# A window-attention block on one core: v projected as pairs of half-height matmuls in two banks, and the split of q and k moved behind the parts of the maxima

## The chip, the core and the metric

The kernel runs on one core of a Trainium2 chip. The metric is device time in microseconds. A core has TensorE (PE, matmuls; its weight loads are listed as PEld), VectorE (DVE), ScalarE (ACT), GpSimd (POOL) and SyncE (SP), which here only issues DMAs. Each engine executes its own instructions in the order written, and waits on semaphores for the others.

## The reference

A shifted-window attention block with its MLP, on x of 8 images of 16 x 128 positions and 32 channels; a window is 4 x 32 = 128 positions, an image has 16 windows, there are 4 heads of 8 channels.

```python
y = layernorm(x, g1, b1); y = roll(y, (-2, -2)); xw = windows(y)          # 128 windows of 128 tokens
q, k, v = split(xw @ qkv_w + qkv_b);  q = q * SCALE
attn = einsum('bhid,bhjd->bhij', q, k) + bias + mask
o = einsum('bhij,bhjd->bhid', softmax(attn), v)
x = x + roll(unwindow(o @ proj_w + proj_b), (2, 2))
z = layernorm(x, g2, b2)
return x + gelu(z @ fc1_w + fc1_b) @ fc2_w + fc2_b
```

## The kernel before

All images stay in SBUF with the 128 tokens of a window on the partitions. A **pair** is two windows with their four heads; there are 64 pairs, 8 per image. The loop runs over steps p from -4 to 63, and step p is step s = p % 8 of image b = p // 8. Every engine has its own copy of the loop, written out by hand, and the order of the `if` lines in it is the order of its instructions.

What a step does: TensorE makes the scores of pair p + 4 with rows i on the partitions in ps1 (`bias_s1`, `scores_s1`); VectorE reduces them to negated row maxima (`row_max`, L406), which frees ps1. Every second step TensorE transposes the maxima of two pairs into the first 16 partitions of Q1 (`transpose_max`, L720). ScalarE takes their bfloat16 high part (`high_max`, m_hi, L589), VectorE the rest (`middle_max`, m_mid, L412), and SyncE sends both into the spare rows of q_rows (`send_max`). Two steps later the scores of that pair are made again, transposed, in ps2 (`bias_s2` L758, `scores_s2` L771), with the maxima subtracted by the matmul itself. ScalarE exponentiates them (`exponential`, L594), which frees ps2. TensorE multiplies with v (`weighted_values`, L791), two steps behind.

Beside this runs the preparation of a later image n = b + 2, and the rest of the block for an earlier one. q and k need three bfloat16 parts. In steps 1 and 3 ScalarE takes the high part (`high_part`) of the two halves, from Q1 and Q0. VectorE subtracts it (`remainder`, L397; the first half in step 1, the second in step 4), ScalarE takes the middle part (`middle_part`, L578; steps 2 and 4), GpSimd the low part (`low_part`, L311; steps 2 and 5), and SyncE scatters and gathers them through DRAM. In step 5 TensorE projects v of image b + 1 into Q0 (`project_v`, L708), which has to wait until the second remainder has read Q0, and ScalarE copies it into va (`values`, L583). `wv` is block diagonal: four copies of the 32 x 32 matrix, for four windows side by side in the partitions.

Normalization has a chain of its own: VectorE sums (`means` L367, L369; `variances` L375, L377), GpSimd centres, takes the power for rstd (L297, 2.9 us) and scales, ScalarE squares (L556). After the attention, TensorE turns the outputs around (L859, L865), projects them (L871, after ScalarE's copy onT), and VectorE adds them to x (L428). pq is one PSUM tensor of two banks, Q0 and Q1, shared by the transpositions, the projections of q, k and v and the maxima. After step 63 comes the MLP of all images.

Of the kernel before, what the change touches and what calls it, by code (L numbers as in the profile page):

```python
# [43 lines left out]
def swin_kernel(nc, x, params, rel_i_in, rel_j_in, aux_in, scratch, out):  # L44
# [3 lines left out]
    with ExitStack() as ctx:  # L48
# [313 lines left out]
        def _(dve):  # L362
# [143 lines left out]
            for p in range(FIRST, PAIRS):  # L506
# [7 lines left out]
                if p % 4 == 2 and 0 <= (p - 6) // 4 < OCTETS:  # L514
                    normalize((p - 6) // 4)
                if p >= 0 and n < B and s in (1, 4):
                    remainder(n, s // 4, (Q1, Q0)[s // 4])
                if s == 4 and 0 <= b - 1 < B:
# [6 lines left out]
                if p % 2 == 0 and 0 <= (p + 2) // 2 < GROUPS:  # L525
                    middle_max((p + 2) // 2)
                if 0 <= p + LEAD < PAIRS:
                    row_max(p + LEAD)
# [22 lines left out]
        def _(act):  # L551
# [28 lines left out]
            def values(n):  # L580
                act.wait_ge(vp_done, n + 1)
                after(act, av_done, PPI * (n - 1))
                act.activation(va[:, n % 2, 16:].rearrange("p (n c) -> p n c", c=32)[:, :, 0:HD],  # L583
                               Q0.rearrange("p (n c) -> p n c", c=HD), ACT.Copy).then_inc(va_done, 1)

# [55 lines left out]
            for p in range(FIRST, PAIRS):  # L641
                b, s = p // PPI, p % PPI
                n = b + 2
                if p >= 0 and n < B:
                    if s == 0:
                        copy_yT(n, Q0)
                    if s in (1, 3):
                        high_part(n, s // 2, (Q1, Q0)[s // 2])
                    if s in (2, 4):
                        middle_part(n, s // 2 - 1)  # L650
                if p % 4 == 3 and 0 <= (p - 7) // 4 < OCTETS:
# [15 lines left out]
                if p % 2 == 0 and 0 <= (p + 2) // 2 < GROUPS:  # L667
                    high_max((p + 2) // 2)
                if 0 <= p < PAIRS:
                    exponential(p)  # L670
# [13 lines left out]
        def _(pe):  # L684
# [21 lines left out]
            def project_v(n):  # L706
                for g in range(NG):
                    mm = pe.matmul(Q0[:, 128 * g:128 * (g + 1)], yT[:, n % 2, 128 * g:128 * (g + 1)], wv[:],  # L708
                                   start=True, stop=True)
                mm.then_inc(vp_done, 1)  # L710

            def transpose_max(k):
                pe.wait_ge(max_done, 2 * k + 2)
                if k:
                    pe.wait_ge(mmid_done, k)
                if k % 4 == 2 and 2 <= (k + 2) // 4 + 1 < B:
                    pe.wait_ge(rest_done, 2 * ((k + 2) // 4 + 1) + 1)
                else:
                    pe.wait_ge(yT_done, 2)
                pe.transpose(Q1[0:16, 0:TOK], negm[:, k % 2, :], P("ident")).then_inc(mT_done, 1)  # L720
# [56 lines left out]
            def weighted_values(j):  # L777
                b = j // PPI
                if j % PPI == 0:
                    pe.wait_ge(va_done, b + 1)  # L780
                if j % 4 == 0:
# [93 lines left out]
            for p in range(FIRST, PAIRS):  # L875
# [6 lines left out]
                if p >= 0 and n < B:  # L882
                    if s == 0:
                        pe.wait_ge(va_done, n - 1)
                        after(pe, yT2_done, n - 4)
                        transpose_first(n, Q0)
                    if s == 1:
                        pe.wait_ge(mmid_done, (p - 1 + 2) // 2 + 1)
                        project_qk(n, (Q0, Q1))
                if p % 4 == 2 and 0 <= (p - 6) // 4 < OCTETS:  # L890
                    tokens_first((p - 6) // 4)
                if s == 5 and 1 <= b + 1 < B:
                    if n < B:
                        pe.wait_ge(rest_done, 2 * n + 2)
                    else:
                        pe.wait_ge(yT2_done, b - 2)
                    project_v(b + 1)
                if s == 7 and 0 <= b - 2 < B - 3:
                    pe.wait_ge(va_done, min(b + 2, B))
                    transpose_second(b - 2, Q0)  # L900
# [161 lines left out]
```

## Time and profile before

| | |
|---|---|
| median of 3 runs | 262.0 us (261.79 to 262.4) |
| the profiled execution | 262.69 us, its span 260.9 us |
| granted TensorE clock, mean | 0.99 |
| loop (first row maxima to last) | about 37 to 225 us |

In the rows, a line of the timeline is one run of like instructions: start in us, length in us, engine, line, operation, output <- inputs, count; in brackets the idle time of the engine before it and what ended that. The length of a run of matmuls reaches to its last modelled end, which lies inside the next run, so starts are what one subtracts.

### The profile page before, as it was taken

How to read it: one execution, taken by the hardware profiler on the slowest of the kernel's cores; microseconds unless marked ns; L12 is line 12 of the kernel's file. 1: busy time of each engine (PE TensorE's matmuls, PEld its weight loads, DVE VectorE, ACT ScalarE, POOL GpSimd, SP SyncE). 2: the span in 40 equal slices, each digit the busy share in tenths (PEclk: the TensorE clock that was granted, in tenths of full speed). 3: DMA queues.
4: the chain of work that ended last, by engine and by line, in shares of the span. 5: the costliest groups of instructions: out<-in, count | busy, mean ns of one | idle time of the engine just before them, and what ended most of it. 6: DMA issues, size and time to landing. Idle time of an engine off the chain costs nothing.

```text
span 260.9 us, 8073 instructions
## 1 busy us (share of the span) xinstructions
PE 215.0 (82%) x3336; PEld 122.3 (47%) x3336; DVE 170.0 (65%) x263; ACT 149.1 (57%) x222; POOL 113.3 (43%) x78
## 2 busy tenths in 40 slices
PE   0249105979999999999999999999999998898673
PEld 0116002436656555665666566566566564432221
DVE  5744764577588687858868786777676663384243
ACT  1342800467577566667757766766556566956460
POOL 8462458123630982487098248531600701616000
PEclk9999999999999999999999999999999999999798
DMA  7915443532550542245154124405500000012112
GB/s 225 205 43 184 138 134 101 159 93 91 164 155 19 184 145 89 83 139 158 47 185 142 49 95 154 126 9 183 166 26 5 4 4 1 3 40 83 40 47 113
DMA packets 24843, 26.30 MB, mean 101 GB/s; under 512 B 3732, under 2 KB 22292, under 8 KB 24596
## 3 DMA queue, kind: packets, MB, share of 16 engines
q1 hardware_dynamic: 23704, 24.82, 30.7%
q10 hardware_dynamic: 1104, 0.99, 1.4%
q8 instruction: 26, 0.43, 0.7%
q14 instruction: 9, 0.07, 0.1%
HBM read 17.14 MB, written 8.39 MB: 98 GB/s over the span
## 4 chain that ended last, share of the span: by engine, by line
issue 35%; PE 34%; POOL 19%; ACT 4%; DVE 3%; DMA 3%; ACTq 1%; POOLq 0%; DVEq 0%
POOL rstd L297 6%; PE pav L791 5%; PE ps L758 4%; POOL parts L311 4%; POOL xc L289 4%; PE pav L820 3%; PE ps L771 3%; PE ps L808 3%; PE ps L726 3%; PE pch L832 2%; POOL yn L304 2%; PE pch L871 2%; POOL X L317 2%; ACT prob L594 2%; PE pch L859 2%
## 5 line engine op out<-in xcount | busy, mean ns | idle before, releaser
L406 DVE TENSOR_REDUCE negm<-ps 128x8 f32<-128x1024 f32 x64 | 78.1, 1220 | 32.0 <-PE ps L744 31.9
L594 ACT ACTIVATE prob<-ps 128x1024 f32<-128x1024 f32 x64 | 65.4, 1021 | 28.5 <-PE ps L771 28.5
L297 POOL TENSOR_TENSOR rstd<-var,neghalf 128x16 f32<-128x16 f32 x16 | 46.6, 2913 | 67.9 <-DVE var L377 67.9
L758 PE MATMUL ps<-rel_j,id_b 96*32 96x512 bf16 x512 | 39.9, 385 | 2.3 <-ACT prob L594 2.3
L791 PE MATMUL pav<-prob,va 128*32 128x128 f32 x1024 | 41.0, 279 | 0.0
L726 PE MATMUL ps<-rel_i,ident_b 64*64 64x512 bf16 x256 | 27.4, 418 | 14.1 <-DVE negm L406 12.3
L791 PEld LDWEIGHTS pav<-prob,va 128*32 128x32 f32 x1024 | 24.1, 109 | 12.3 <-issue 5.5
L311 POOL TENSOR_TENSOR parts<-rest,parts 128x512 bf16<-128x512 f32 x16 | 18.8, 1180 | 21.4 <-ACT parts L578 21.4
L289 POOL TENSOR_TENSOR xc<-X,mean 128x512 f32<-128x512 f32 x13 | 13.6, 1048 | 29.4 <-DVE mean L369 29.1
L744 PE MATMUL ps<-k_rows,q_rows 64*128 64x128 bf16 x512 | 25.9, 223 | 0.0
L771 PE MATMUL ps<-q_rows,k_rows 64*128 64x128 bf16 x512 | 25.7, 220 | 0.1
L589 ACT ACTIVATE m_hi<-pq 16x128 bf16<-16x128 f32 x32 | 8.4, 263 | 25.3 <-PE pq L720 25.3
L726 PEld LDWEIGHTS ps<-rel_i,ident_b 64*64 64x64 bf16 x256 | 7.3, 105 | 31.5 <-DVE negm L406 22.6
L771 PEld LDWEIGHTS ps<-q_rows,k_rows 64*128 64x128 bf16 x512 | 14.5, 95 | 15.5 <-issue 14.9
L744 PEld LDWEIGHTS ps<-k_rows,q_rows 64*128 64x128 bf16 x512 | 17.4, 97 | 1.7 <-issue 1.3
L556 ACT ACTIVATE sq<-xc 128x512 f32<-128x512 f32 x15 | 9.4, 626 | 15.1 <-POOL xc L289 8.5
L375 DVE TENSOR_REDUCE vsum<-sq 128x16 f32<-128x512 f32 x16 | 10.9, 678 | 9.8 <-ACT sq L556 9.7
L758 PEld LDWEIGHTS ps<-rel_j,id_b 96*32 96x32 bf16 x512 | 12.4, 97 | 8.0 <-ACT prob L594 7.6
L304 POOL TENSOR_TENSOR yn<-xc,rstd 128x512 f32<-128x512 f32 x14 | 14.7, 1048 | 2.0 <-PE pch L696 1.3
L412 DVE TENSOR_TENSOR m_mid<-pq,m_hi 16x128 bf16<-16x128 f32 x32 | 8.9, 277 | 9.7 <-ACT m_hi L589 8.0
L578 ACT ACTIVATE parts<-rest 128x512 bf16<-128x512 f32 x16 | 9.9, 625 | 6.9 <-DVE rest L397 6.0
L871 PE MATMUL pch<-par,onT 128*128 128x128 f32 x64 | 11.4, 300 | 2.0 <-ACT onT L655 1.5
(104 smaller groups left out, 312.6 us busy)
## 6 DMA issues: line engine op xcount, KB each, us to landing
slots<-parts SPq DMA_DIRECT2D x24, 256.0 KB, 2.3
q_rows<-slots SPq DMA_DIRECT2D x42, 128.0 KB
k_rows<-slots SPq DMA_DIRECT2D x42, 128.0 KB
X<-x_tok SPq DMA_DIRECT2D x8, 256.0 KB, 3.6
y_tok<-res SPq DMA_DIRECT2D x8, 256.0 KB, 2.0
prob<-bias_j SPq DMA_DIRECT2D x3, 256.0 KB, 6.9
k_rows<-slots ACTq DMA_DIRECT2D x12, 64.0 KB, 2.3
q_rows<-slots SPq DMA_DIRECT2D x12, 64.0 KB, 2.4
```

The source lines that it names most:

```text
L289: pool.tensor_tensor(per_window(xc[:, i, :]), per_window(img(n)), mean[:, i, :].unsqueeze(2).to_broadcast([128, WPI, C]), ALU.subtract).th ...
L297: pool.tensor_tensor(rstd[:, i, :], var[:, i, :], neghalf[:], ALU.pow).then_inc(rstd_done[i], 1)
L304: pool.tensor_tensor(per_window(yn[:, i, :]), per_window(xc[:, i, :]), rstd[:, i, :].unsqueeze(2).to_broadcast([128, WPI, C]), ALU.mult).t ...
L311: pool.tensor_tensor(parts[:, n % 2, LOW, 1 - i, :], rest[:, 1 - i, :], parts[:, n % 2, MID, 1 - i, :], ALU.subtract).then_inc(lo_done, 1)
L406: dve.tensor_reduce(dst, ps1[:].rearrange("p (a u n) -> p a u n", u=2, n=TOK), AX.X, ALU.max, negate=True).then_inc(max_done, 1)
L594: act.activation(prob[:, j % NPROB, :], ps2[:], ACT.Exp).then_inc(exp_done, 1)
L726: pe.matmul(ps1[64 * c:64 * (c + 1), 512 * e:512 * (e + 1)], ident_b[64 * e:64 * (e + 1), 64 * e:64 * (e + 1)], rel_i[64 * e:64 * (e + 1), ...
L744: mm = pe.matmul(ps1[:, 512 * e + at:512 * e + at + TOK], q_rows[64 * e:64 * e + 64, b % NBUF, rows], k_rows[64 * e:64 * e + 64, b % NBUF, ...
L758: pe.matmul(ps2[32 * c:32 * (c + 1), 512 * e:512 * (e + 1)], id3_b[0:96, :], rel_j[0:96, c, e].unsqueeze(2).to_broadcast([96, 2, 2, TOK]), ...
L771: mm = pe.matmul(ps2[:, 512 * e + at:512 * e + at + TOK], k_rows[64 * e:64 * e + 64, b % NBUF, rows], q_rows[64 * e:64 * e + 64, b % NBUF, ...
L791: mm = pe.matmul(pav[32 * h:32 * (h + 1), 128 * (j % 4):128 * (j % 4 + 1)], va[:, b % 2, at:at + 32], prob[:, j % NPROB, src:src + 128], s ...
L871: mm = pe.matmul(pch[:, 128 * t:128 * (t + 1)], onT[:, 128 * t:128 * (t + 1)], P("wp"), start=True, stop=True)
```

## The change

`project_v` makes two matmuls where it made one: rows 0 to 63 of yT and the upper left block of wv into Q0, rows 64 to 127 and the lower right block into Q1, 64 output columns each. `values` reads the two banks with two activations, so va_done counts two for each image. `project_v` in step 5 also waits for m_mid of step 4, which reads Q1, and the transposition of the maxima in step 6 waits for both copies of v. In VectorE's step 4 the remainder moves from ahead of the means and `middle_max` to behind them, ahead of the row maxima. In ScalarE's steps 2 and 4 the middle part moves from ahead of `high_max` to behind it, ahead of the exponentials.

```diff
@@ VectorE's loop
-                if p >= 0 and n < B and s in (1, 4):
-                    remainder(n, s // 4, (Q1, Q0)[s // 4])
+                if p >= 0 and n < B and s == 1:
+                    remainder(n, 0, Q1)
                 if s == 4 and 0 <= b - 1 < B:
                     dve.wait_ge(x2_done, 2 * b)
                     means(second_norm(b - 1), b - 1)
...
                 if p % 2 == 0 and 0 <= (p + 2) // 2 < GROUPS:
                     middle_max((p + 2) // 2)
+                if p >= 0 and n < B and s == 4:
+                    remainder(n, 1, Q0)
                 if 0 <= p + LEAD < PAIRS:
                     row_max(p + LEAD)
@@ ScalarE
             def values(n):
                 act.wait_ge(vp_done, n + 1)
                 after(act, av_done, PPI * (n - 1))
-                act.activation(va[:, n % 2, 16:].rearrange("p (n c) -> p n c", c=32)[:, :, 0:HD],
-                               Q0.rearrange("p (n c) -> p n c", c=HD), ACT.Copy).then_inc(va_done, 1)
+                to = va[:, n % 2, 16:].rearrange("p (g u n c) -> p u g n c", g=NG, u=2, c=32)
+                for u in range(2):
+                    act.activation(to[:, u, :, :, 0:HD],
+                                   (Q0, Q1)[u][:, 0:256].rearrange("p (g n c) -> p g n c", g=NG, c=HD),
+                                   ACT.Copy).then_inc(va_done, 1)
...
                     if s in (1, 3):
                         high_part(n, s // 2, (Q1, Q0)[s // 2])
-                    if s in (2, 4):
-                        middle_part(n, s // 2 - 1)
...
                     high_max((p + 2) // 2)
+                if 0 <= p and n < B and s in (2, 4):
+                    middle_part(n, s // 2 - 1)
                 if 0 <= p < PAIRS:
                     exponential(p)
@@ TensorE
             def project_v(n):
                 for g in range(NG):
-                    mm = pe.matmul(Q0[:, 128 * g:128 * (g + 1)], yT[:, n % 2, 128 * g:128 * (g + 1)], wv[:],
-                                   start=True, stop=True)
+                    for u in range(2):
+                        rows = slice(64 * u, 64 * (u + 1))
+                        mm = pe.matmul((Q0, Q1)[u][:, 64 * g:64 * (g + 1)], yT[rows, n % 2, 128 * g:128 * (g + 1)],
+                                       wv[rows, rows], start=True, stop=True)
                 mm.then_inc(vp_done, 1)
 
             def transpose_max(k):
                 pe.wait_ge(max_done, 2 * k + 2)
                 if k:
                     pe.wait_ge(mmid_done, k)
+                if k % 4 == 0:
+                    pe.wait_ge(va_done, 2 * (k // 4 + 1))
...
                         pe.wait_ge(rest_done, 2 * n + 2)
                     else:
                         pe.wait_ge(yT2_done, b - 2)
+                    pe.wait_ge(mmid_done, (p - 1 + 2) // 2 + 1)
                     project_v(b + 1)
```

The other waits on va_done are doubled in count.

## Rows read from the trace of the kernel before

**Rows 1.** The page's first part: busy time, share of span, instructions.
```profile
PE 215.0 (82%) x3336; PEld 122.3 (47%) x3336; DVE 170.0 (65%) x263; ACT 149.1 (57%) x222; POOL 113.3 (43%) x78
```

**Rows 2.** Timeline, steps 20 and 21 (steps 4 and 5 of image 2).
```profile
103.81 0.41 DVE L428 TENSOR_TENSOR X<-X,pch 128x256 f32<-128x256 f32 x1
104.14 0.74 DVE L397 SCALAR_TENSOR_TENSOR rest<-pq,qk_bias,parts 128x512 f32<-128x512 f32 x1
...
104.92 0.63 ACT L578 ACTIVATE parts<-rest 128x512 bf16<-128x512 f32 x1 [0.93 <-DVE rest L397]
...
104.99 0.39 PE L744 MATMUL ps<-k_rows,q_rows 64*128 64x128 bf16 x8
...
105.31 1.16 PE L708 MATMUL pq<-wv_s,yT 128*128 128x128 f32 x8
105.46 0.25 ACT L589 ACTIVATE m_hi<-pq 16x128 bf16<-16x128 f32 x1
...
105.61 1.00 ACT L594 ACTIVATE prob<-ps 128x1024 f32<-128x1024 f32 x1
...
105.74 0.28 DVE L412 TENSOR_TENSOR m_mid<-pq,m_hi 16x128 bf16<-16x128 f32 x1
105.94 1.20 DVE L406 TENSOR_REDUCE negm<-ps 128x8 f32<-128x1024 f32 x1
...
106.40 0.65 PE L791 MATMUL pav<-prob,va 128*32 128x128 f32 x16
106.52 0.59 ACT L583 ACTIVATE va<-pq 128x512 f32<-128x512 f32 x1
106.75 0.23 PEld L758 LDWEIGHTS ps<-rel_j,id_b 96*32 96x32 bf16 x8
...
108.19 1.02 ACT L594 ACTIVATE prob<-ps 128x1024 f32<-128x1024 f32 x1 [0.48 <-PE ps L771]
```

**Rows 3.** Timeline, steps 4 and 5 (image 0).
```profile
59.45 0.28 PE L720 MATMUL pq<-par,negm 128*16 128x128 f32 x1
...
60.66 1.00 ACT L594 ACTIVATE prob<-ps 128x1024 f32<-128x1024 f32 x1
...
61.99 0.23 PEld L758 LDWEIGHTS ps<-rel_j,id_b 96*32 96x32 bf16 x8
```

**Rows 4.** Timeline of VectorE, steps 52 and 53 (image 6).
```profile
194.13 0.69 DVE L367 TENSOR_REDUCE ssum<-X 128x16 f32<-128x512 f32 x1
194.85 0.17 DVE L369 TENSOR_SCALAR mean<-ssum 128x16 f32<-128x16 f32 x1
194.93 0.28 DVE L412 TENSOR_TENSOR m_mid<-pq,m_hi 16x128 bf16<-16x128 f32 x1
...
198.28 1.23 DVE L406 TENSOR_REDUCE negm<-ps 128x8 f32<-128x1024 f32 x1 [1.70 <-PE ps L744]
```

**Rows 5.** Timeline of TensorE, from image 1 to 2 and from 2 to 3.
```profile
91.24 0.71 PE L871 MATMUL pch<-par,onT 128*128 128x128 f32 x4 [0.59 <-ACT onT L655]
...
113.39 0.39 PE L744 MATMUL ps<-k_rows,q_rows 64*128 64x128 bf16 x8
...
114.06 0.71 PE L871 MATMUL pch<-par,onT 128*128 128x128 f32 x4 [0.29 <-ACT onT L655]
```

**Rows 6.** Timeline, steps 25 and 26 (steps 1 and 2 of image 3).
```profile
118.73 1.27 POOL L317 TENSOR_TENSOR X<-X,pb_full 128x512 f32<-128x512 f32 x1
119.30 0.74 DVE L369 TENSOR_SCALAR mean<-ssum 128x16 f32<-128x16 f32 x1
...
121.87 0.09 PEld L720 LDWEIGHTS pq<-par,negm 128*16 128x16 f32 x1 [0.62 <-DVE negm L406]
```

**Rows 7.** Timeline of ScalarE, step 18 (step 2 of image 2).
```profile
99.37 0.27 ACT L589 ACTIVATE m_hi<-pq 16x128 bf16<-16x128 f32 x1 [0.69 <-PE pq L720]
...
100.04 1.02 ACT L594 ACTIVATE prob<-ps 128x1024 f32<-128x1024 f32 x1 [0.41 <-PE ps L771]
```

**Rows 8.** Timeline of TensorE, step 26 (step 2 of image 3).
```profile
122.63 0.23 PEld L771 LDWEIGHTS ps<-q_rows,k_rows 64*128 64x128 bf16 x8 [0.44 <-DMA q_rows<-m_mid]
```

More of the change, by code:

```diff
@@ L779, in weighted_values @@
                 if j % PPI == 0:
-                    pe.wait_ge(va_done, b + 1)
+                    pe.wait_ge(va_done, 2 * (b + 1))
                 if j % 4 == 0:
@@ L883, in _ @@
                     if s == 0:
-                        pe.wait_ge(va_done, n - 1)
+                        pe.wait_ge(va_done, 2 * (n - 1))
                         after(pe, yT2_done, n - 4)
@@ L896, in _ @@
                         pe.wait_ge(yT2_done, b - 2)
+                    pe.wait_ge(mmid_done, (p - 1 + 2) // 2 + 1)
                     project_v(b + 1)
                 if s == 7 and 0 <= b - 2 < B - 3:
-                    pe.wait_ge(va_done, min(b + 2, B))
+                    pe.wait_ge(va_done, 2 * min(b + 2, B))
                     transpose_second(b - 2, Q0)
```

## The prediction

> **What bounds the kernel now.** I read the page's busy shares first, then the timeline of one whole image engine by engine, then for each wait the row that ended it. TensorE is busy 82% of the span and the next engine, VectorE, 65% [rows 1], and most of its idle time lies in the start and the MLP. So the middle of the kernel (steps 0 to 63, eight per image) is a TensorE chain, interrupted wherever something it needs comes late. Three things are candidates in every step: the exponentials of the step before (they free ps2, which the j-side bias refills), the row maxima of the step before (they free ps1), and the matmuls themselves.
>
> Rows 2 show steps 4 and 5 of image 2 (steps 20 and 21). ScalarE takes the middle part at 104.92, m_hi at 105.46, the exponentials at 105.61; TensorE starts the projection of v at 105.31, the weighted values at 106.40, and loads the j-side bias at 106.75. The exponentials end at 106.61, that is 0.14 us ahead of that load. A release takes some 0.04 us (the middle part starts at 104.92 after the remainder's end at 104.88 [rows 2]); towards TensorE I take 0.06, an estimate from that. The margin is 0.08 us. So step 5 is a TensorE step, with the exponentials right under it. Anything that delays them by more than 0.08 us delays the step.
>
> **The order on ScalarE and VectorE in step 4.** This is the part that decides. In the changed code the remainder stands behind m_mid on VectorE and the middle part behind m_hi on ScalarE, but the middle part still stands ahead of the exponentials, and the exponentials read nothing that the remainder makes. Worked out for image 2 from the clock of the trace:
> - VectorE: the add of the attention ends at 104.22 (103.81 + 0.41) [rows 2]. Without a remainder behind it the sums, means and m_mid follow as in step 52, where ssum starts 0.04 after such an add, the mean 0.72 after that, m_mid 0.08 after that [rows 4]. So ssum 104.26, mean 104.98, m_mid 105.06. m_mid needs m_hi, which is then no longer behind the middle part: the transposition of the maxima takes 0.28 and starts at 59.45 in image 0 [rows 3]; m_hi can start 0.32 after such a start, in image 2 long before 105.06, since the transposition stands ahead of the scores at 104.99. The remainder starts 0.20 after m_mid (m_mid and the row maxima start 0.20 apart today [rows 2]), at 105.26, and ends at 106.00 (0.74 long, today 104.14 to 104.88). The row maxima start at about 105.93, today 105.94: VectorE has the same sum of work, so nothing is won or lost there.
> - ScalarE: the middle part starts at 106.04 (today 0.04 after the remainder's end), and what follows it starts 0.54 later [rows 2]: the exponentials at 106.58 instead of 105.61, end 107.59 instead of 106.61.
> - TensorE: the projection waits for the remainder (it overwrites Q0, which the remainder reads): 106.05 instead of 105.31. Its added wait for m_mid is over by then. The projection and the weighted values fill the time up to the exponentials' end. The j-side bias loads at 107.65 instead of 106.75: **0.90 us late**, and the row maxima (ended 107.14) no longer matter.
> Image 0 has no means in step 4. There m_hi comes at 59.77, m_mid 60.07, remainder 60.27 to 61.01, middle part 61.05, exponentials 61.59 instead of 60.66, end 62.60, bias load 62.66 instead of 61.99: 0.67 us late [rows 3]. The other images with a remainder (1, 3, 4, 5) repeat image 2's spacing to 0.02 us.
>
> **The projection of v.** It was eight instructions (two passes for each float32 matmul), 1.09 us to the start of the next work [rows 2]; it becomes sixteen, each half as many columns and half as many rows. The trace has no float32 matmul of 64 rows and 64 columns. Below: the scores are also pairs in two row halves, with 128 bfloat16 columns, eight in 0.39 us [rows 2], so sixteen in 0.8 us. Above: each at its present 0.136 us, 2.2 us. I take 0.8, since the scores have the same pairing and load the same 128 columns of weights. In steps 5 of images 0 to 5 it gains nothing: the projection could last 1.25 us before the weighted values (0.35) would run into the exponentials' end. In image 6 (step 53) there is no remainder; there the row maxima sat idle 1.70 us waiting for the scores [rows 4], so TensorE is the path and the gain is 1.09 - 0.80 = 0.3 us. Projection 0 lies in the start, where TensorE waits for others; I put it at nothing: the normalization and the split of images 0 and 1 are what the first scores wait for. If that cover were gone it would be the same 0.3 us of gain, or up to 1.1 of loss.
> The Trainium skill (TensorEngine Tiling (Array Packing), Instruction Overhead) speaks against this part: it puts about 60 cycles on each matmul and warns against tiling out of a dimension that is already small. An estimate from that figure is 8 added instructions at some 25 ns, 0.2 us, so a projection of 1.0 and a gain of 0.1 in step 53; no row here shows it, and it would add 0.2 us to the sum below.
>
> **The two reads of v.** One copy of 512 columns (0.59 us [rows 2]) becomes two of 256 columns: between 0.6 and 1.2 us. They stand after the exponentials of step 4 (now to 107.59), then comes the copy of oT (0.60), then the exponentials of step 5, which today wait 0.48 us for their scores [rows 2] and will be due 0.9 later. The two copies and oT end by 108.7 to 109.3 and the scores are there at 109.1: hidden, or at worst 0.2 us. The wait of the next transposition into Q1 for these copies is a whole step away: nothing.
>
> **Step 2.** m_hi already waited for its transposition there, so it comes no earlier. The middle part moves from before m_hi to between m_hi and the exponentials. Today the exponentials start 0.67 after m_hi [rows 7]; with it between they start 0.17 + 0.53 = 0.70 after. TensorE waits for these exponentials in step 3, so 0.03 us each, 0.15 in all. The last part on GpSimd comes 1.5 us later and nothing behind it is due before step 5.
>
> **SyncE.** It sends the maxima of step 4 about 0.9 us earlier and can scatter the high part earlier; the middle scatter waits for a middle part that ends 1.1 us later (106.67 for 105.55), with the gathers of the high part queued behind it, but two sends and the high scatter stand ahead of it, so I take the queue as no later than today. It would cost something only if TensorE came to wait for it. TensorE waited for this queue once, in step 26 [rows 8], 0.44 us of which about half is the usual gap: at most 0.2 us to be had.
>
> **What is taken back.** A delay of TensorE shrinks where TensorE is later waiting for a chain that did not move. The means and variances of steps 4 and 5 stay in place on VectorE (row maxima at 105.93), so GpSimd's rstd, xc and ScalarE's sq and onT stay in place too.
> - Start of the next image: the projection out waits for onT behind sq. In image 2 the last scores start at 113.39, work could follow 0.32 later at 113.71, and it starts at 114.06: 0.35 slack. In image 1 the idle is 0.59 instead of 0.29, so 0.66 [rows 5]. Images 1 to 4 have this; 0 and 5 have not.
> - Step 1: the mean takes 0.74 us against 0.17 elsewhere, because it ends only as GpSimd's add (118.73 + 1.27) does; the row maxima are late for that, and the next transposition sits idle 0.62 instead of 0.42 [rows 4, 6]: 0.20 slack in images 2, 3 and 4, where GpSimd's add has not moved. The Trainium skill (SBUF — State Buffer) has an exclusive port pair of VectorE and GpSimd behind such a pair of rows; by that rule, too, the mean's end stays tied to GpSimd's.
> So by image of origin: image 0 +0.67; image 1 +0.90 - 0.66 - 0.20 = +0.04; image 2 +0.90 - 0.35 - 0.20 - 0.20 (the wait of step 26) = +0.15; image 3 +0.90 - 0.35 - 0.20 = +0.35; image 4 +0.90 - 0.35 = +0.55; image 5 +0.90. Sum 2.66. With step 2 (+0.15) and step 53 (-0.30): **+2.5 us**. The profiled execution of before took 262.69 us (span 260.9), so it would become 265.2; against the median of 262.0 that is **264.5 us**.
>
> **Rivals.**
> - A, the delay is absorbed: all the waits above give more slack than I read (GpSimd's chain restores the rhythm once per image) and image 0's loss sinks in the next image, leaving 0 to 0.5 us: 262.3. For it: such waits stand in images 1 to 4 [rows 5, 6]. Against: they hold 0.35 to 0.86 us each, and images 0 and 5 have none. 8%.
> - B, faster: TensorE's own work decides step 5 and the seven projections in the loop count in full, 7 x 0.3 = 2.1 us: 259.9. It holds only if the exponentials of step 4 still end by about 106.7, so if the remainder ended before some 105.1 on VectorE. By the order of the code it cannot; a partial form, with a gain in queue time of SyncE on top, is what is left. 7%.
> - C, larger loss: the pairs don't overlap and the projection takes 2.2 us, 0.95 beyond the 1.25 that is covered, and the two copies cost 0.2: six times up to 0.9, and 1.1 in step 53, less what is taken back (about half): +3.5 on top, 268. Or nothing is taken back: 0.67 + 5 x 0.90 = 5.2, 267. 10%.
> - The change doing nothing is no rival: the order of each engine is written out.
> The forecast itself holds the remaining 75%, between 263.3 and 266.
>
> **How the numbers follow.** Range 263.1 to 266.4: down by the absorption of images 2 to 4 being complete (-1.0) with 0.3 left for scatter, up by half of the taken-back time failing to come (1.2) and a dearer projection (0.7). Faster or slower by over 0.2%, 0.5 us, is about what a measurement of this kernel can tell from no change. Slower: forecast and C, 0.85. Same: A, 0.08. Faster: B, 0.07.
>
> **What the profile after would show.** Right: in step 4 of images 0 to 5 the exponentials start about 0.95 us later against the row maxima of the step before, with the middle part directly ahead of them and ScalarE idle "until the remainder"; TensorE idle before the projection for 0.7 us and before the j-side bias, released by the exponentials; the onT waits at the start of images 2 to 5 gone or shorter; the projection's group sixteen a time in 0.8 us. Wrong: exponentials of step 4 where they were, the projection over 1.25 us, or a new TensorE wait for a copy of v or for a DMA.

## The result, and the profile after

| | before | after |
|---|---|---|
| median of 6 runs | 261.89 us (261.18 to 262.40) | 264.44 us (263.06 to 265.32) |
| ratio, with its 95% interval | | 1.0089 [1.0054, 1.0124] |
| profiled execution | 262.69 us | 265.32 us |
| its span, mean granted clock | 260.9 us, 0.99 | 263.5 us, 0.983 |
| row maxima of step 3 to those of step 59, in the profiled execution | 156.19 us | 158.16 us |

The change makes the kernel slower by 0.9%, with bounds of 0.54% and 1.24%. The first part of the page after (busy time, share of the span, instructions) answers to [rows 1]:

```profile
PE 216.1 (82%) x3400; PEld 122.4 (46%) x3400; DVE 169.0 (64%) x263; ACT 149.4 (57%) x230; POOL 113.4 (43%) x78
```

The engines are as busy as before to about 1 us; VectorE, which had work moved, is no busier. So the time came as waits. To find them I took the start of each of the 64 row maxima in both traces and looked at how the difference (after less before) grows from one step to the next. One thing has to be settled first, because the two spans differ by 2.7 us and not all of it is the change's doing:

- Before the loop the changed kernel is ahead: the first parts of image 0's keys on ScalarE start at 24.30 us after a wait for a DMA of 3.37 us, and at 24.88 after 3.95 before. By step 3 it is 0.75 ahead. That moves from run to run (step 3's row maxima start between 56.70 and 58.32 us in the fourteen traces of this case).
- From step 3 to step 59 it loses **1.97 us**. This is the loop, and here the traces repeat each other to about 0.02 us in stretches that an edit doesn't touch, so I use this stretch as the measure below.
- Behind the loop, in the MLP at the end, it loses 1.45 more. The windows of both traces over the end show where (columns: length, busy time and count of PE, PEld, DVE, ACT, POOL, granted clock, DMA share, GB/s), first before:

```profile
241.00:246.00 5.00, 2.25 (x16) 1.09 (x20) 1.19 (x2) 2.60 (x3) 0.00 (x0) 0.92 0.01 2
246.00:251.00 5.00, 4.22 (x28) 1.41 (x22) 0.94 (x2) 2.72 (x3) 0.00 (x0) 0.74 0.27 102
```
then after:
```profile
241.00:246.00 5.00, 2.21 (x18) 1.04 (x15) 0.75 (x1) 2.61 (x3) 0.34 (x1) 0.82 0.00 0
246.00:251.00 5.00, 4.99 (x21) 1.42 (x20) 1.44 (x2) 1.02 (x2) 0.00 (x0) 0.50 0.14 52
```

The granted clock of TensorE falls there in both (0.50 is the lower of its two levels, 1.2 GHz), around the same wait of 2.79 us for yT. The timeline of TensorE, before and after:

```profile
243.75 0.63 PE L832 MATMUL pch<-par,mT 128*128 128x128 f32 x4 [2.79 <-ACT yT L567]
244.31 1.14 PE L820 MATMUL pav<-q_rows,par 128*32 128x512 f32 x8
```
```profile
244.97 1.09 PE L841 MATMUL pch<-par,mT 128*128 128x128 f32 x4 [2.79 <-ACT yT L569]
245.99 1.94 PE L829 MATMUL pav<-q_rows,par 128*32 128x512 f32 x8
```

Before, the clock is still 1.00 from 244 to 245 us, over 1.2 us behind the end of the wait, 0.58 from 245 to 246, and full again at 248.6. After, it has fallen before the wait ends, is 0.50 from 245 on, and full again only at 251.0. From the end of the wait to the next group of matmuls (L808, L817 after) the twelve matmuls take 1.63 us before and 2.88 after, which is 1.25 of the 1.45. From the row maxima of step 59 to the end of that wait both kernels take the same 29.51 us, and no line of the change touches this part. Nor does the clock there follow the change: the same twelve matmuls take 1.59 us in the kernel with the change's order alone and 2.88 in the one with ScalarE's move alone (both below). From step 59 to the end the fourteen traces take between 45.1 and 48.4 us.

The steps in which the loop's 1.97 us arise are in the table, as the amount by which the difference has grown from one image's steps 4 and 5 to the next image's (each figure rounded by itself), against the prediction's list:

| origin | predicted | measured: lost in steps 4 and 5, taken back later | net |
|---|---|---|---|
| image 0 | +0.67 | +0.53, nothing | +0.53 |
| image 1 | +0.04 | +0.77, -0.67 start of image 2, -0.12 step 17 | -0.02 |
| image 2 | +0.15 | +0.76, -0.37 step 24, -0.42 steps 25 and 26 | -0.02 |
| image 3 | +0.35 | +0.77, -0.37 step 32, -0.20 steps 33 and 34 | +0.20 |
| image 4 | +0.55 | +0.76, -0.37 step 40 | +0.39 |
| image 5 | +0.90 | +0.77, nothing | +0.77 |
| step 53 | -0.30 | | +0.12 |
| step 2 of all | +0.15 | under 0.01 in all | 0.00 |
| sum | 2.5 | | 1.97 |

Image 2, whose rows of before are [rows 2], looks like this after (timeline: start, length, engine, line, and in brackets the idle time before and what ended it):

```profile
103.57 0.41 DVE L428 TENSOR_TENSOR X<-X,pch 128x256 f32<-128x256 f32 x1
...
104.28 0.27 ACT L594 ACTIVATE m_hi<-pq 16x128 bf16<-16x128 f32 x1 [0.53 <-PE pq L729]
...
104.75 0.39 PE L753 MATMUL ps<-k_rows,q_rows 64*128 64x128 bf16 x8
104.82 0.28 DVE L412 TENSOR_TENSOR m_mid<-pq,m_hi 16x128 bf16<-16x128 f32 x1
105.02 0.73 DVE L397 SCALAR_TENSOR_TENSOR rest<-pq,qk_bias,parts 128x512 f32<-128x512 f32 x1
105.68 1.20 DVE L406 TENSOR_REDUCE negm<-ps 128x8 f32<-128x1024 f32 x1
105.79 0.63 ACT L580 ACTIVATE parts<-rest 128x512 bf16<-128x512 f32 x1 [1.24 <-DVE rest L397]
...
105.81 1.11 PE L715 MATMUL pq<-wv_s,yT 64*128 64x64 f32 x16 [0.67 <-DVE rest L397]
106.32 1.01 ACT L599 ACTIVATE prob<-ps 128x1024 f32<-128x1024 f32 x1
...
106.84 0.64 PE L800 MATMUL pav<-prob,va 128*32 128x128 f32 x16
107.23 0.65 ACT L587 ACTIVATE va<-pq 128x256 f32<-128x256 f32 x2
107.38 0.12 PEld L767 LDWEIGHTS ps<-rel_j,id_b 96*32 96x32 bf16 x8 [0.16 <-ACT prob L599]
107.38 0.61 PE L767 MATMUL ps<-rel_j,id_b 96*32 96x512 bf16 x8
```

Here the changed kernel is 0.24 us ahead of the old one (the add of the attention starts at 103.57 for 103.81). VectorE does the remainder 0.20 after m_mid; ScalarE sits idle 1.24 us until the remainder is there, and only then do the middle part and the exponentials follow; TensorE waits 0.67 for the remainder ahead of the projection and 0.16 for the exponentials ahead of the j-side bias.

### The profile page after: what moved, and what is told of

It reads as the page before. It is cut to its first block, busy times and chain, and to the rows that moved or that the text cites. A ratio compares the mean times of both kernels' runs of the same rounds, so it can differ in the third digit from the quotient of the medians.

```text
span 263.5 us, 8223 instructions
## 1 busy us (share of the span) xinstructions
PE 216.1 (82%) x3400; PEld 122.4 (46%) x3400; DVE 169.0 (64%) x263; ACT 149.4 (57%) x230; POOL 113.4 (43%) x78
## 4 chain that ended last, share of the span: by engine, by line
PE 69%; DVE 12%; issue 6%; ACT 5%; DMA 3%; POOL 3%; ACTq 1%; DVEq 0%; POOLq 0%
PE pav L800 11%; PE ps L767 10%; PE ps L735 8%; PE ps L780 7%; PE ps L753 5%; PE pch L868 4%; PE pq L715 3%; PE ps L817 3%; PE pch L880 3%; PE pav L829 3%; DVE rest L397 2%; DVE negm L406 2%; PE pq L707 2%; PE pq L729 2%; PE pch L874 2%
## 5 line engine op out<-in xcount | busy, mean ns | idle before, releaser
L767 PEld LDWEIGHTS ps<-rel_j,id_b 96*32 96x32 bf16 x512 | 11.7, 96 | 8.7 <-ACT prob L599 8.3
L715 PE MATMUL pq<-wv_s,yT 64*128 64x64 f32 x128 | 9.6, 294 | 3.9 <-DVE rest L397 3.8
```

What stands on the lines that cost most here:

```text
L715: mm = pe.matmul((Q0, Q1)[u][:, 64 * g:64 * (g + 1)], yT[rows, n % 2, 128 * g:128 * (g + 1)], wv[rows, rows], start=True, stop=True)
L767: pe.matmul(ps2[32 * c:32 * (c + 1), 512 * e:512 * (e + 1)], id3_b[0:96, :], rel_j[0:96, c, e].unsqueeze(2).to_broadcast([96, 2, 2, TOK]), ...
```

## The experiments

Each kernel is told by the time from the row maxima of step 3 to those of step 59 (before 156.19, after 158.16) and by its timed ratio to before. The stretch is read from one trace of each kernel; the intervals of the ratios are 0.5 to 0.8% wide, so they alone don't tell kernels apart that differ by less than about 1 us.

**Order alone.** The moves on VectorE and ScalarE of the change's diff, with v projected and read as before.

```diff
@@ before, VectorE
-                if p >= 0 and n < B and s in (1, 4):
-                    remainder(n, s // 4, (Q1, Q0)[s // 4])
+                if p >= 0 and n < B and s == 1:
+                    remainder(n, 0, Q1)
...
+                if p >= 0 and n < B and s == 4:
+                    remainder(n, 1, Q0)
                 if 0 <= p + LEAD < PAIRS:
@@ before, ScalarE
-                    if s in (2, 4):
-                        middle_part(n, s // 2 - 1)
...
+                if 0 <= p and n < B and s in (2, 4):
+                    middle_part(n, s // 2 - 1)
                 if 0 <= p < PAIRS:
                     exponential(p)
```

> The kernel before with the order of the change alone: remainder behind m_mid on VectorE in step 4, middle part behind m_hi on ScalarE in steps 2 and 4; v is projected as before, into Q0 alone. I compare the loop by the time from the first to the last row maxima in the profile (176.70 us before, 178.47 us changed, +1.77). Theory (the exponentials of step 4 stand behind a late remainder): they start about 0.95 us later, the j-side bias matmuls of step 5 start 0.75 to 0.8 late in images 1 to 5, and the loop is 1.6 to 1.8 us longer, as in the whole change. Rival (the pairs and their second bank cost the time): 0 to 0.3 us.

Measured: 158.02 us, 1.83 more than before; ratio 1.0064 [1.0030, 1.0099]. From the first row maxima to the last, which is what the expectation was stated in, it lost only 0.95, less than the 1.6 to 1.8 expected; but that stretch also holds steps 0 and 1, where the granted clock comes up to full at another moment in each trace: from 48.1 us on in this one, from 50.6 in before. It is 0.90 shorter in those two steps alone. From step 3 on its differences are those of the changed kernel to 0.02 us in every step up to 52; the only one that is missing is the 0.12 of step 53. The order makes 1.83 of the 1.97.

**Pairs alone.** The pairs, the two copies and the added waits, in the old order of VectorE and ScalarE.

```diff
@@ after, VectorE
-                if p >= 0 and n < B and s == 1:
-                    remainder(n, 0, Q1)
+                if p >= 0 and n < B and s in (1, 4):
+                    remainder(n, s // 4, (Q1, Q0)[s // 4])
...
-                if p >= 0 and n < B and s == 4:
-                    remainder(n, 1, Q0)
@@ after, ScalarE
+                    if s in (2, 4):
+                        middle_part(n, s // 2 - 1)
...
-                if 0 <= p and n < B and s in (2, 4):
-                    middle_part(n, s // 2 - 1)
```

> The changed kernel with the order of before on VectorE and ScalarE: pairs into Q0 and Q1, two copies and the new waits alone. Theory: the exponentials of step 4 start where they did before, but the projection now waits for m_mid, which in this order ends at 106.02 in image 2's time where the projection started at 105.31: 0.7 us late at the j-side bias in images 1 to 5, 0.5 in image 0, 0.12 in step 53, part of it taken back as in the whole change; the loop 1.5 to 1.8 us longer. So each half costs what both cost together. Rival (the order is the only cause): 0.1 us.

Measured: 159.38 us, 3.19 more than before; ratio 1.0073 [1.0038, 1.0108]. From the first row maxima to the last it is 2.55 more, where 1.5 to 1.8 were expected. Step 5 loses 0.61 us in image 0 and 0.8 in the others, as much as with the new order, but by another wait. The timeline of this kernel in step 20, and in step 18:

```profile
106.21 0.28 DVE L412 TENSOR_TENSOR m_mid<-pq,m_hi 16x128 bf16<-16x128 f32 x1
...
106.64 1.11 PE L713 MATMUL pq<-wv_s,yT 64*128 64x64 f32 x16 [0.79 <-DVE m_mid L412]
```
```profile
100.07 0.40 PE L778 MATMUL ps<-q_rows,k_rows 64*128 64x128 bf16 x8 [0.88 <-DMA q_rows<-m_mid]
```

With the old order m_mid comes last, and the second bank of the pairs makes the projection wait for it. In step 18 TensorE sits idle 0.88 us until the maxima that SyncE sent have landed; 0.95 of the loss is from there, and without it 2.24 are left. I had not foreseen that wait. The trace shows how it came about. SyncE's waits between 80 and 104 us, in the kernel before and in this one:

```profile
SPq L221 <- DMA slots<-parts: 1.2, 1, 1.2
```
```profile
SPq L221 <- DMA slots<-parts: 3.6, 1, 3.6
```

The scatter of a split part that SyncE issues at 83.61 lands 4.5 us later; the one in before (84.09) lands 2.1 us later. The gathers queue behind it, a later scatter is as slow (4.4 us for 2.1), and m_mid of step 16 is sent at 98.43 instead of 96.47. The same scatter takes 2.1 or 2.2 us in twelve of the fourteen traces and 4.1 in one more, and every trace has scatters of 3 us and more elsewhere, so the 0.95 may be this execution's and not the edit's; why a transfer is slow is not shown. So the pairs are no gain that the order spoils: they lose on their own (2.24 us even so), and in the new order they cost 0.14 more than the order does.

**Exponentials first.** The changed kernel with the middle part behind the exponentials: it tells whether the late exponentials are the loss.

```diff
-                if 0 <= p and n < B and s in (2, 4):
-                    middle_part(n, s // 2 - 1)
                 if 0 <= p < PAIRS:
                     exponential(p)
+                if 0 <= p and n < B and s in (2, 4):
+                    middle_part(n, s // 2 - 1)
```

> The changed kernel with the middle part behind the exponentials instead of ahead of them in steps 2 and 4. Theory: the exponentials of step 4 no longer wait for the remainder and start about 0.4 us earlier than in the kernel before, but the projection of v still waits for it (0.74 us late, 1.04 long), so the bias matmuls of step 5 are 0.7 late instead of 0.78: the loop 1.3 to 1.6 us longer than before, against 1.77 in the whole change. Rival (the exponentials are the only cause, the projection's wait is hidden): the loop as before or shorter, 0 us.

Measured: 157.79 us, 1.60 more than before, 0.37 less than after; ratio 1.0047 [1.0012, 1.0081]. In the measure of the expectation, first row maxima to last, it is 1.13 more, a little under the 1.3 to 1.6 expected. Its timeline in step 20:

```profile
104.57 1.02 ACT L599 ACTIVATE prob<-ps 128x1024 f32<-128x1024 f32 x1 [0.41 <-PE ps L780]
...
105.43 1.11 PE L715 MATMUL pq<-wv_s,yT 64*128 64x64 f32 x16 [0.68 <-DVE rest L397]
...
106.93 0.62 PE L767 MATMUL ps<-rel_j,id_b 96*32 96x512 bf16 x8
```

The exponentials start early, end at 105.59, and TensorE loses nearly the same: 0.45 us in image 0 and 0.69 in the others, where the changed kernel loses 0.53 and 0.77. The projection's wait for the remainder is a second cause of the same loss, only 0.08 us behind the first. This qualifies the prediction's picture, in which "the projection and the weighted values fill the time up to the exponentials' end".

**ScalarE's move alone.** Before, with the middle part behind m_hi, and VectorE untouched.

```diff
-                    if s in (2, 4):
-                        middle_part(n, s // 2 - 1)
...
+                if 0 <= p and n < B and s in (2, 4):
+                    middle_part(n, s // 2 - 1)
                 if 0 <= p < PAIRS:
                     exponential(p)
```

> The kernel before with ScalarE's part of the order alone: the middle part behind m_hi in steps 2 and 4, the remainder where it was. Theory: the remainder is done at 104.88 in image 2's time, m_hi comes 0.9 us earlier and the exponentials of step 4 some 0.15 us earlier, which TensorE doesn't need; step 2 costs 0.03 each: the loop 0 to 0.2 us longer. Rival (ScalarE's order by itself delays TensorE): over 0.5 us longer. If SyncE's earlier sends were worth anything, it would be shorter than before.

Measured: 155.41 us, 0.78 **less** than before; ratio 0.9971 [0.9945, 0.9997]. My theory missed this: it had 0 to 0.2 us of loss and no gain in it. Timeline of step 20, beside [rows 2]:

```profile
104.42 0.27 ACT L589 ACTIVATE m_hi<-pq 16x128 bf16<-16x128 f32 x1 [0.54 <-PE pq L720]
104.81 0.63 ACT L578 ACTIVATE parts<-rest 128x512 bf16<-128x512 f32 x1
105.35 1.00 ACT L594 ACTIVATE prob<-ps 128x1024 f32<-128x1024 f32 x1
105.49 0.27 DVE L412 TENSOR_TENSOR m_mid<-pq,m_hi 16x128 bf16<-16x128 f32 x1
105.69 1.20 DVE L406 TENSOR_REDUCE negm<-ps 128x8 f32<-128x1024 f32 x1
```

m_hi no longer stands behind the middle part, so m_mid and the row maxima behind it start 0.15 us earlier against the kernel before, and with them the variances and GpSimd's chain. TensorE gets 0.14 or 0.15 back wherever it waits for onT (steps 15, 23, 31, 39), and 0.21 in step 26, where it waited for a DMA. So ScalarE's half of the order is a gain, and the loss comes with the remainder's place on VectorE: 155.41 without it, 158.02 with it. VectorE's half cannot be run without ScalarE's. The remainder would wait behind m_mid for m_hi, m_hi behind the middle part on ScalarE, and the middle part for the remainder.

**Is the delay taken back by chains that didn't move?** I moved the chain behind onT out of the way: the squares one place later on ScalarE and the variances behind the row maxima, in the kernel before and in the kernel after.

```diff
@@ ScalarE
-                if s == 6 and 0 <= b - 1 < B:
+                if s == 7 and 0 <= b - 1 < B:
                     square(second_norm(b - 1))
@@ VectorE
-                if s == 7 and 0 <= b - 1 < B:
-                    variances(second_norm(b - 1))
...
                     row_max(p + LEAD)
+                if s == 7 and 0 <= b - 1 < B:
+                    variances(second_norm(b - 1))
```

> The kernel before with the waits taken out in which I say the delays were taken back: the square of the second normalization moves on ScalarE from the end of step 6 to the end of step 7, behind onT and the exponentials, and its variances on VectorE from ahead of step 7's row maxima to behind them. I compare the time from the row maxima of step 3 to those of step 59 (156.19 us before, +1.97 in the changed kernel). Theory: TensorE no longer waits for onT at the start of images 2 to 5 and the row maxima of step 7 don't wait for the square; 0.66 + 3 x 0.35 us are gained, 1.4 to 2.0 us shorter, unless GpSimd's later rstd then collides with the mean of step 1. Rival (those waits were not on the path): no change.

> The changed kernel with the same removal of waits. Theory: the six delays of the change (0.53 + 5 x 0.78 and 0.12 in step 53, 4.5 us) now stay in full but for what step 1 takes back (up to 0.2 in three images), so this kernel is 3.9 to 4.5 us longer than the same removal in the kernel before, where the change itself was 1.97 longer than before. Rival (the waits don't take back anything, the delays themselves differ by image): a difference of 2.0 us as before.

Measured: before with it 155.04 (ratio 0.9989 [0.9960, 1.0017]), after with it 158.08 (1.0062 [1.0025, 1.0099]). The first is 1.15 us shorter than before, under the 1.4 to 2.0 that I expected, and the interval of its timed ratio includes 1. The gap grows from 1.97 to 3.04 us, less than the 3.9 to 4.5 that I expected. Three waits in the altered before still took time back. One is DMA's in step 26 (0.7 us). One is in step 16, where TensorE's transposition of yn waits for GpSimd: it starts 0.82 us after the projection ahead of it and 0.14 after yn's end, and in the altered after 0.55 after that projection. The third is the mean of step 17, which lies beside an operation of GpSimd. The rows, all of the altered before:

```profile
121.22 0.40 PE L771 MATMUL ps<-q_rows,k_rows 64*128 64x128 bf16 x8 [0.64 <-DMA q_rows<-m_mid]
```
```profile
89.02 1.05 POOL L304 TENSOR_TENSOR yn<-xc,rstd 128x512 f32<-128x512 f32 x1
...
90.21 0.63 PE L689 MATMUL pq<-par,yn 128*128 128x128 f32 x4
```
```profile
94.80 1.05 POOL L304 TENSOR_TENSOR yn<-xc,rstd 128x512 f32<-128x512 f32 x1
94.91 0.97 DVE L369 TENSOR_SCALAR mean<-ssum 128x16 f32<-128x16 f32 x1
```

So I took the first of them away as well, with SyncE's two `gather` calls for the middle part moved from step 7 to step 0 of the next image, behind the sending of the maxima.

```diff
@@ SyncE, on top of the edit above
                 if s == 0 and 1 <= b + 1 < B:
+                    gather(b + 1, MID, 0)
+                    gather(b + 1, MID, 1)
                     gather(b + 1, LOW, 0)
...
-                    if s == 7:
-                        gather(n, MID, 0)
-                        gather(n, MID, 1)
```

> The kernel before with the square moved (155.04 us from step 3 to 59) and one more wait taken out: SyncE issues the four gathers of the middle parts behind the sends of the maxima of step 0 instead of ahead of them. In the square's kernel TensorE waited 0.64 us in step 26 for m_mid to land, and that took back 0.7 us of what two images had gained. Theory: 154.3 to 154.5 us. Rival (DMA queues are the limit, not SyncE's order): 155.0 us, with the wait in another step.

> The changed kernel with the same two removals. It had no DMA wait in the loop with the square moved (158.08 us), because it ran later: so no gain from this, 158.0 to 158.2 us. The change then costs 3.6 to 3.9 us between step 3 and 59, against 3.05 with the square's move alone and 1.97 as it is: all but what the mean of step 1 takes back (0.7 in image 1). Rival: the cost stays at 3.0.

Measured: before with both 154.34 (ratio 0.9956 [0.9928, 0.9985]), after with both 158.06 (1.0059 [1.0025, 1.0093]). The gap is 3.72 us, inside the 3.6 to 3.9 expected. By step, the delays of images 2 to 5 now stay in full; of image 1's, 0.74 is still taken back: 0.31 in step 16, where TensorE waits for yn, and 0.43 in steps 17 and 18, where the mean stands beside GpSimd. The same change to the order and the projection costs 1.97, 3.04 or 3.72 us, by how much idle time the kernel has elsewhere to swallow it.

**The price of the pairs.** Two versions of the changed kernel with less work in the projection, each run once. The first loads 64 columns of yT as weights instead of 128 and writes 64 rows of the output; the second moves 32 columns of wv through instead of 64.

```diff
@@ 64 columns of weights
-                        mm = pe.matmul((Q0, Q1)[u][:, 64 * g:64 * (g + 1)], yT[rows, n % 2, 128 * g:128 * (g + 1)],
+                        mm = pe.matmul((Q0, Q1)[u][0:64, 64 * g:64 * (g + 1)], yT[rows, n % 2, 128 * g:128 * g + 64],
@@ 32 moving columns
-                        mm = pe.matmul((Q0, Q1)[u][:, 64 * g:64 * (g + 1)], yT[rows, n % 2, 128 * g:128 * (g + 1)],
-                                       wv[rows, rows], start=True, stop=True)
+                        mm = pe.matmul((Q0, Q1)[u][:, 64 * g:64 * g + 32], yT[rows, n % 2, 128 * g:128 * (g + 1)],
+                                       wv[rows, 64 * u:64 * u + 32], start=True, stop=True)
```

> The price of the sixteen instructions of the projection: the changed kernel with half the weights in each, 64 of the 128 columns of yT (the other 64 tokens of each window get no new v, that part of the computation is left out). If the loading of the weights sets the 1.04 us that the pairs take in step 53, it falls to 0.5 to 0.7 us; if the moving columns or a fixed cost for each instruction set it, it stays above 0.95.

> The price of the projection from the other side: the changed kernel with 32 instead of 64 moving columns in each matmul of the projection, and full weights (half of the columns of v are left out). If the weights set it, the 1.04 us of step 53 stay; if the moving columns do, it falls to 0.6; a fixed cost for each instruction leaves it as it is both here and with half the weights.

The timelines of step 53, where nothing else holds TensorE: the time from the projection's start to that of the weighted values is its price. Changed kernel, then 64 columns of weights, then 32 moving columns:

```profile
196.02 0.27 DVE L412 TENSOR_TENSOR m_mid<-pq,m_hi 16x128 bf16<-16x128 f32 x1
...
196.44 1.11 PE L715 MATMUL pq<-wv_s,yT 64*128 64x64 f32 x16
...
197.48 0.64 PE L800 MATMUL pav<-prob,va 128*32 128x128 f32 x16
```
```profile
195.85 0.68 PE L715 MATMUL pq<-wv_s,yT 64*64 64x64 f32 x16
...
196.46 0.65 PE L800 MATMUL pav<-prob,va 128*32 128x128 f32 x16
```
```profile
196.70 1.08 PE L715 MATMUL pq<-wv_s,yT 64*128 64x32 f32 x16
...
197.71 0.65 PE L800 MATMUL pav<-prob,va 128*32 128x128 f32 x16
```

1.04 us, 0.61 us, 1.01 us. Half the moving columns save 0.03; half the columns of weights save 0.43. So the columns of weights set the price. The rows of the weights don't: here are all the weight loads of the projection in the kernel before, in the changed kernel and in the one with 64 columns (nanoseconds of one load, least, median and most):

```profile
L708 PEld LDWEIGHTS pq<-wv_s,yT x64: 186/192/334, 23.2 to 196.0; 128*128 128x128 f32 x64
```
```profile
L715 PEld LDWEIGHTS pq<-wv_s,yT x128: 182/188/334, 22.2 to 197.2; 64*128 64x128 f32 x128
```
```profile
L715 PEld LDWEIGHTS pq<-wv_s,yT x128: 129/135/223, 23.2 to 196.3; 64*64 64x64 f32 x128
```

A load of 64 rows takes as long as one of 128 (188 and 192 ns). The records of step 53 one by one show the rest. In the old projection a pass starts every 0.112 us; in the new one the two passes of a pair start 0.036 apart, and a pair starts every 0.112 us too. With 64 columns of weights it is a pair every 0.058, with 32 moving columns again every 0.112. Eight pairs replace eight passes at the same pace, and the 0.05 us between 1.09 and 1.04 lies in the first and the last of them.

**Better versions.** ScalarE's move alone gained, and so, in the stretch from step 3 to 59, did the two moves that I had made only as a probe. Together, first without and then with the gathers:

```diff
@@ before, ScalarE, with the edits of the squares, the variances (and the gathers) above
-                    if s in (2, 4):
-                        middle_part(n, s // 2 - 1)
...
+                if 0 <= p and n < B and s in (2, 4):
+                    middle_part(n, s // 2 - 1)
```

> The kernel before with both what the runs point to: ScalarE's middle part behind m_hi (0.78 us shorter from step 3 to 59, ratio 0.997) and the square and variances moved behind step 7's work. If the first gained by making the row maxima of step 4, and with them the GpSimd chain that ends in the square, 0.15 us earlier, its gain falls away when that chain is no longer waited for: the same as the square's move alone to 0.2 us. If it gained on TensorE's own path, the two add up: 0.6 to 0.8 us shorter than the square's move alone.

> Everything that the runs point to in one kernel, on the base of the kernel before: ScalarE's middle part behind m_hi, square and variances behind step 7's work, sends ahead of the middle gathers. The kernel without the last was at 154.37 us from step 3 to 59 and waited 0.6 us for m_mid once: 153.6 to 153.9 us expected, 2.3 to 2.6 us less than the kernel before (156.19), ratio 0.990 in the timed runs. If the sends' move delays a gather that the next image needs, 154.4 or more.

Measured: 154.37 us and 153.75 us, that is 1.82 and 2.44 less than before; timed 0.9912 [0.9873, 0.9950] and 0.9925 [0.9895, 0.9956], medians 259.53 and 260.55. Both beat both kernels; the timed runs don't tell them apart. Once the squares' chain had been moved I thought the 0.15 of ScalarE's order might have nothing left to act on. It brought 0.67 instead (155.04 to 154.37): 0.14 in step 16, where TensorE waits less for yn, 0.43 in steps 17 and 18, where the mean now just escapes GpSimd, and most of the rest in step 26. Timeline of the version without the gathers, beside the 0.97 above:

```profile
95.02 0.17 DVE L369 TENSOR_SCALAR mean<-ssum 128x16 f32<-128x16 f32 x1
95.05 1.05 POOL L304 TENSOR_TENSOR yn<-xc,rstd 128x512 f32<-128x512 f32 x1
```

## Why the prediction was right, and where it was not

The prediction said 264.5 us, slower; the median is 264.44. The sign and the mechanism hold, and so do nearly all the places. The closeness of the total is luck: the loop was predicted at +2.5 and is +1.97 in the profiled executions. Even that is closer than its terms, since 0.8 us of loss too much in the six images and 0.15 in step 2 stand against 0.4 of gain too much in step 53. The remaining 0.6 of the medians' 2.55 is in no step of mine; the start and the clock at the end of the kernel vary by such amounts between traces, and the ratio's interval alone spans 1.8 us.

- **VectorE and ScalarE in step 4: right.** With the 0.24 us that the trace is ahead in image 2, the prediction's times become m_mid 104.82, remainder 105.02, projection 105.81, exponentials 106.34, j-side load 107.41. Measured: 104.82, 105.02, 105.81, 106.32, 107.38.
- **0.90 us late: the mechanism right, the size off by 0.13.** The load of the bias is 0.87 late, but its matmuls only 0.76: they started 0.11 after the load before, in the row below, and start with it now. I measured the delay at the load; the path runs through the matmul. The same 0.13 is most of the miss in every image (0.53 for 0.67 in image 0).

```profile
106.86 0.62 PE L758 MATMUL ps<-rel_j,id_b 96*32 96x512 bf16 x8
```

- **The exponentials as the only cause: too simple.** The kernel with the exponentials first shows the projection's wait for the remainder 0.08 us behind. The sum didn't suffer, since the later of the two counts. But a reader who would mend the change by moving the exponentials would get back 0.37 of 1.97.
- **The pairs at 0.80 us: wrong, 1.04.** The step that failed is "the scores have the same pairing and load the same 128 columns of weights". The scores are bfloat16. A load of 64 rows by 128 columns is recorded with 0.094 us for them and 0.188 for the float32 projection, and their pairs start 0.056 us apart, those of the projection 0.112. (The 0.39 us for eight scores was a length, too; by starts they take 0.32.) In step 53 the gain is 0.05, not 0.3. The estimate that I made from the Trainium skill (TensorEngine Tiling (Array Packing), Instruction Overhead), 1.0 us with a gain of 0.1, came much nearer. Its reason does not: a fixed cost for each matmul would not fall with the columns of the weights, from 1.04 us for the sixteen to 0.61.
- **"Its added wait for m_mid is over by then": wrong in step 53.** I worked that out for the steps with a remainder and carried it to the one without. There m_mid starts at 196.02, only after the sums and the mean, ends at 196.29, and the projection starts at 196.44. The step lost 0.12 although the pairs gain 0.05, so the wait costs 0.17 there; the kernel with the order alone, which has neither wait nor pairs, loses nothing in that step.
- **Projection 0: right, nothing.** It takes 1.74 us for 1.87 in the start, and TensorE then waits 1.34 us for VectorE where it waited 1.80.
- **The two copies of v: right, hidden.** They take 0.65 us together for 0.59, and nothing waits for them; the exponentials of step 5 still wait 0.35 for their scores (0.48 before).
- **Step 2: right.** The exponentials start 0.69 us after m_hi (99.82 and 99.13), and in [rows 7] 0.67.
- **SyncE: right, small.** TensorE's wait in step 26 [rows 8] is down to its usual 0.23:

```profile
122.37 0.23 PEld L780 LDWEIGHTS ps<-q_rows,k_rows 64*128 64x128 bf16 x8 [0.23 <-issue]
```

- **What is taken back: right in places and sizes.** The waits for onT of [rows 5] are gone after (90.81 to 91.13 and 113.91 to 114.22 from the last scores to the next work, 0.32 and 0.31, as the prediction said work could follow), and the mean of [rows 6] takes 0.32 us for 0.74. Only the mean of step 17 gave back less than I put down, 0.12 for 0.20:

```profile
90.81 0.39 PE L753 MATMUL ps<-k_rows,q_rows 64*128 64x128 bf16 x8
91.13 0.71 PE L880 MATMUL pch<-par,onT 128*128 128x128 f32 x4
...
113.91 0.39 PE L753 MATMUL ps<-k_rows,q_rows 64*128 64x128 bf16 x8
114.22 0.71 PE L880 MATMUL pch<-par,onT 128*128 128x128 f32 x4
...
119.44 0.32 DVE L369 TENSOR_SCALAR mean<-ssum 128x16 f32<-128x16 f32 x1
```

The kernels with these waits removed show that they are the cause, not only the place: 3.72 us instead of 1.97.
- **The rivals.** A (absorbed, 262.3) held in images 1 and 2 alone; images 0, 3, 4 and 5 kept 0.20 to 0.77 each. B (faster) fails at its own condition, since the exponentials of step 4 end at 107.33 and not by 106.7. C fails as the pairs cost 1.04 and not 2.2, and as more than half of the delays are taken back.

What stays open: why the clock at the end falls earlier and stays low longer in some executions; the last 0.2 us of the loss behind the loop; and why the scatters were slow in the trace of the kernel with the pairs alone, and whether its edit had a part in that.

## What to carry to other kernels

A step that is moved behind another engine's result delays everything queued behind it and everything that waits for its bank: work out the start of each, and take the later. Then follow the delay forward to each place where the bound engine waits for something that did not move, since it shrinks there, and price it at the instruction that does the work, not at its weight load. And when two edits come as one change, ask of each half alone: here one half of the reordering (ScalarE's) was a gain, and with two later places for the squares and the variances it makes a kernel 0.9% faster than before (0.5 to 1.3%).

## What the runs showed of the hardware that I had not expected

- A float32 matmul with 128 columns of weights goes by those columns here, with 64 rows as with 128: a pass of 128 rows starts every 0.112 us, and so does a pair of passes of 64 rows with 64 moving columns, or with 32. With 64 columns of weights it is a pair every 0.058. Splitting the rows in two halves gives two passes at the price of one and so gains nothing but 0.05 us at the ends.
- The same mean of 128x16 takes 0.17 us alone and 0.32, 0.74 or 0.97 beside a GpSimd operation on two tensors that started first, and it ends about when that does (95.88 and 95.85 in step 17). When it started 0.03 us ahead of GpSimd it took 0.17. The rule of the Trainium skill (SBUF — State Buffer), a port pair that one of VectorE and GpSimd holds at a time, agrees. In step 17 the mean started 0.11 us behind GpSimd in one kernel and 0.03 ahead of it in another, and that was worth 0.43.
- Around the same idle time of 2.79 us in the MLP, the granted clock fell over 1.2 us behind its end in one execution and ahead of its end in another; the twelve matmuls behind it took 1.63 and 2.88 us.
